# Two-layer vision tower on one core: the place of the square roots, the signed inverse and the selection in the first factorisation

## The reference, cut to what matters

```
p = unfold(x)                                  # 64 images, 51 patches of 64 x 25
h = gelu(p @ weight + bias)                    # C = 64 channels
n = layernorm(h)
q, k, v = split(n @ w_qkv.T + b_qkv)           # 8 heads of 8 channels
qgr, _ = qr(q);  kgr, _ = qr(k)                # per image and head: 51 x 8
grass = (qgr @ kgr.T) ** 2 * grassman_scale
dots  = q @ k.T
a = batchnorm(concat(dots * scale, dots ** 2 * riem_scale, grass))
a = softmax(conv_1x1(a))
h = h + (a @ v) @ w_proj.T + b_proj
h = h + mixture_of_experts(layernorm(h))       # 6 experts, the best 2
```

## Time and profile before

| | us |
|---|---|
| median of three runs (334.08 to 338.35) | 334.38 |
| the profiled execution, its own time | 336.93 |
| its span, from the first to the last instruction | 334.4 |
| TensorE matmul busy | 283.7 (85%) |
| VectorE busy | 201.1 (60%) |
| ScalarE busy | 172.0 (51%) |
| GpSimd busy | 70.5 (21%) |
| mean granted TensorE clock of the span | 0.911 |

### The profile page before, as it was taken

How to read it: one execution, slowest core, us unless ns; L and a number is a source line. 1 busy time by engine, 2 the same in 40 slices (tenths; PEclk the granted TensorE clock), 3 DMA queues, 4 the chain that set the end, 5 groups by cost and what they waited for, 6 DMA issues and landing times.

```text
span 334.4 us, 11326 instructions
## 1 busy us (share of the span) xinstructions
PE 283.7 (85%) x4854; PEld 199.1 (60%) x4854; DVE 201.1 (60%) x549; ACT 172.0 (51%) x310; POOL 70.5 (21%) x78
## 2 busy tenths in 40 slices
PE   4296999999788578595999999999876899998883
PEld 2176766877557467474788887886755453333331
DVE  1445087967477569788465466575587362465571
ACT  2445363342523156853566885666654565445731
POOL 8001114201103131132178322352200030000000
PEclk9787999999969879789599999999999899559999
DMA  8999960000000000000000000000000000010102
GB/s 226 284 297 269 251 159 2 5 3 4 0 2 2 5 2 2 2 2 2 4 3 4 4 4 2 2 6 2 4 2 0 2 1 2 1 25 2 25 0 50
DMA packets 16848, 13.88 MB, mean 42 GB/s; under 512 B 4128, under 2 KB 16416, under 8 KB 16800
## 3 DMA queue, kind: packets, MB, share of 16 engines
q1 hardware_dynamic: 16800, 13.18, 15.9%
HBM read 12.34 MB, written 0.84 MB: 39 GB/s over the span
## 4 chain that ended last, share of the span: by engine, by line
PE 63%; DVE 17%; ACT 8%; issue 7%; SPq 2%; DMA 2%; POOL 0%; ACTq 0%; DVEq 0%; POOLq 0%
PE banks L1149 10%; PE banks L1424 8%; PE banks L1408 6%; PE banks L1435 5%; PE banks L1449 4%; PE banks L1548 3%; PE banks L1583 3%; PE banks L1532 2%; PE banks L1569 2%; PE banks L1239 2%; DMA pixels<-in_x_dram 2%; PE banks L1155 2%; DVE pixels L918 2%; PE banks L1169 1%; PE banks L1209 1%
## 5 line engine op out<-in xcount | busy, mean ns | idle before, releaser
L1424 PE MATMUL banks<-pixels,convw 64*64 64x204 f32 x768 | 43.4, 358 | 9.9 <-DVE pixels L922 9.9
L309 POOL TENSOR_TENSOR qbd<-q,weights 128x448 f32<-128x448 f32 x32 | 31.4, 984 | 89.6 <-PE banks L1408 89.4
L1149 PE MATMUL banks<-pixels,taps 64*64 64x204 f32 x800 | 40.7, 355 | 9.2 <-DVE pixels L226 6.3
L1149 PEld LDWEIGHTS banks<-pixels,taps 64*64 64x64 f32 x800 | 32.3, 142 | 15.3 <-DVE pixels L226 7.0
L918 DVE TENSOR_REDUCE pixels<-banks 128x8 f32<-128x408 f32 x32 | 18.6, 583 | 35.9 <-PE banks L1424 33.8
L1424 PEld LDWEIGHTS banks<-pixels,convw 64*64 64x64 f32 x768 | 30.1, 143 | 14.5 <-issue 11.4
L1408 PE MATMUL banks<-kbd,qbd 64*64 64x102 f32 x1024 | 33.0, 270 | 2.9 <-issue 1.5
L1408 PEld LDWEIGHTS banks<-kbd,qbd 64*64 64x64 f32 x1024 | 26.3, 144 | 7.6 <-issue 4.3
L284 POOL TENSOR_TENSOR rstd<-var_eps,minus_half 102x8 f32<-102x8 f32 x8 | 13.1, 1639 | 77.2 <-DVE var_eps L710 77.1
L523 ACT ACTIVATE pixels<-banks 128x816 f32<-128x816 f32 x32 | 27.2, 851 | 0.0
L1449 PEld LDWEIGHTS banks<-vbd,pixels 115*51 115x51 f32 x512 | 15.7, 133 | 18.1 <-issue 13.5
(11 more groups left out here) (175 smaller groups left out, 505.0 us busy)
## 6 DMA issues: line engine op xcount, KB each, us to landing
pixels<-in_x_dram SPq DMA_DIRECT2D x16, 434.0 KB, 6.8
pixels<-in_x_dram SPq DMA_DIRECT2D x32, 108.5 KB, 6.9
out_dram<-pixels SPq DMA_DIRECT2D x8, 102.0 KB
weights<-in_w_dram SPq DMA_DIRECT2D x1, 652.0 KB, 8.8
weights<-in_w_dram SPq DMA_DIRECT2D x1, 564.0 KB, 7.8
taps<-in_w_dram SPq DMA_DIRECT2D x1, 416.0 KB, 3.5
```

Source lines behind the costliest of these rows:

```text
L309: pool.tensor_tensor(qbd[u][:, :].rearrange("p (c h i) -> p c h i", c=QB, h=H), qv.unsqueeze(2).to_broadcast([128, QB, H, NI]), w("headmas ...
L1149: last = nc.tensor.matmul(bank[r][64 * s:64 * s + 64, 0:2 * EN], tap(u, r), src, start=(u == 0), stop=(u == PW - 1))
L1424: last = nc.tensor.matmul(bank[2 + r][64 * to:64 * to + 64, 0:4 * N], convw[64 * r:64 * r + 64, k * HI:(k + 1) * HI], src[64 * r:64 * r + ...
```

## The change

Four edits, all around the first factorisation:

- ScalarE gets a new operation `load_roots()`: a square root of one constant column (`eps`) into a new tile `root` of 128 x 1, for which nothing waits. It stands behind `value_tokens(1)`.
- `pivot_roots(0)` moves from behind `center(2)` to ahead of `squares_ln(2)`, directly behind `load_roots()`.
- On VectorE `signed_inverse(0)` comes directly behind signs(7), ahead of `variance_eps(3)`. `variance_eps(3)` follows it, and `scale_ln(3)` moves behind `gram_blocks(8)` and `(9)`.
- On TensorE `select_q_and_k(0)` moves from behind gram(10) to ahead of `broadcast1(3)`.

```diff
+        root = sb("root", [128, 1])
...
+            def load_roots():
+
+                nc.scalar.activation(root[:, :], vec("eps"), ACT.Sqrt).then_inc(S["root_table"], 1)
+
             def pivot_roots(b):
...
             value_tokens(1)
+            load_roots()
+            pivot_roots(0)
             squares_ln(2)
             center(2)
-            pivot_roots(0)
             gelu(3)
...
                 elif j == 4:
                     scale_ln(2)
-                elif j == 6:
-                    variance_eps(3, 3)
-                elif j == 7:
-                    scale_ln(3)
             signed_inverse(0)
+            variance_eps(3, 3)
             gram_blocks(8)
             gram_blocks(9)
+            scale_ln(3)
             q_times_k(0)
...
             gram(9)
+            select_q_and_k(0)
             broadcast1(3)
             tokens(11)
             gram(10)
-            select_q_and_k(0)
             q_and_k(3)
```

More of the change, by code:

```diff
@@ L190, in vit_tower_kernel @@
             q_mm k_mm q_done k_done kbd_k tok_tr v_mm qk_tok_done v_tok_done
-            gram_mm gmask_done cgram_done atop_cp atop_mm g_mm aug_done elim pivots qr_pow lu linv_done sel_mm
+            gram_mm gmask_done cgram_done atop_cp atop_mm g_mm aug_done elim pivots root_table qr_pow lu linv_done sel_mm
             mstep z_mm ik_cp sel_cp z_cp bd_done kp_mm kp_done cvec_mm cvec
```

## The result

| | before | after |
|---|---|---|
| all runs beside each other | 22 runs, median 337.5 us (330.6 to 342.3) | 22 runs, median 331.52 us (326.9 to 336.48) |
| mean of all runs | 337.08 us | 331.41 us |
| the profiled execution | 336.93 us, span 334.4 | 329.21 us, span 326.6 |
| mean granted clock of that span | 0.911 | 0.909 |

The ratio is 0.9896, with a 95% interval of 0.985 to 0.9941: about 1% faster, and clear of no change. That ratio compares only the runs within 1.5% of each kernel's fastest (6 of 22 before, 12 of 22 after); the medians of all runs lie further apart, 331.52 / 337.5 = 0.982. Both are given, since part of the difference is time at the lower clock, and that is not the same in every run.

A forecast was written before the change was run, and what follows sets the result against it. VectorE's order in the first factorisation was taken as the bound; 1.6 (roots), about 3.1 (order) and 0.9 us (clock) made 5.6, discounted to 5.2: 329.2 us from a median of 334.38, range 325.5 to 332.9.

The forecast's parts named there:

- Roots 1.6: ScalarE's earlier pivot root starts VectorE 2.17 us earlier; 1.58 us remain at group 2's scaling, then held by its broadcast.
- The 3.1 of the order: Gain of about 3.1 us up to block_m(0) from reordering signed inverse, gram blocks and selection.
- the 0.9 of the clock: Gain of 0.9 us because TensorE's q and k of group 3 no longer last at half clock.
- The sum: block_m(0) 5.6 us earlier, 4.0 without the earlier half clock; at one in four, 5.2 us, giving 329.2 us.
- How the numbers follow: Range 325.5 to 332.9 us; chances 29% under 327.7, 68% within 2%, 3% above 341.1, only by a doubled E.
- E: Rival: the shift lowers the clock before the experts and keeps it down, up to 8.4 us lost, 337.6 us; 4%.
- Up to 73 us TensorE is simply full: Claim that before the first factorisation's stretch TensorE had no idle time, 41.30 busy of 41.30 us in a window.
- the shift reaches the end: Claim that the second factorisation, steps and experts wait for nothing absolute in time, so the 5.6 us carry through.
- rival C: Later half-clock stretches, from 112 us on, fall elsewhere: one fewer gives 325.9 us (20%), one more 332.5 us (8%).
- The constant's root: New ScalarE operation behind the early table load, priced at 0.20 us, able to gain nothing since nothing reads it.
- B: Rival: TensorE falls to half clock in the new place too; gain 3.6 us, 330.8 us; 12%.
- D: Rival: table switch costs 2.66 us instead of 1.28 (329.6 us), or the norms absorb the rest (332.8 us); 6% together.

The follow-up runs named there:

- e10: Kernel before with only ScalarE's new order (constant's and pivots' roots ahead of the third group's squares), run a second time; 332.15 us, a single execution.
- e5: Kernel before run once more, unchanged, for another trace; 338.72 us, a single execution; 24.94 us from the third group's variance to block_m(0).
- e7: Changed kernel without the constant's root and with the two waits of the Gelu operations swapped; 329.43 us median of 6, ratio 0.9763.
- e3: Changed kernel without load_roots(), the pivots' root still ahead of the squares; 332.03 us median of 4, ratio 0.9852.

## Why the prediction was right or wrong

- **The places of the events in the stretch: right.** Roots 2.17 earlier: 1.05 to -1.19 is 2.24. Scaling of group 2 moved by 1.58: 1.60, and held by the broadcast. Squares still in time for the variance: no idle time before it. Signed inverse within the idle time: 88.94 against 90.30. Selection ahead of the broadcast costs 0.25: 0.18. Product of q and k at 91.8 - 75.40 = 16.4 into the stretch: 16.18. `block_m(0)` at 20.47: 20.14. Gain against that trace 5.6: 5.92. One path was not as worked out: the columns' product, priced at 0.91 us from a row that was partly at half clock, took 0.74 and ended at 97.61, and `block_m(0)` waited for gram block 10 (97.31 and 0.63 us), which the prediction left out of that path. That the two end some 0.3 us apart, so that the number came out, is luck.
- **The shares in it.** Roots 1.6: 1.60, shown (e10 against before). The 3.1 of the order and the 0.9 of the clock can't be compared one by one, since the dip also lengthens the path in which the order's share was counted. Without any dip the forecast was 4.0 in all, so 2.4 for the order; e10 against the changed kernel gives 22.65 - 20.14 = 2.5, and the sum is 4.1. With the dip of the first trace the clock's whole share was 5.6 - 4.0 = 1.6; it was 1.8.
- **The step that failed is the discount in "The sum"**, which took the half clock of 94.4 to 101.0 to be missing in one execution of four and whole in the others, and so made 5.2 of 5.6 and 4.0. The clock's share in that forecast is 1.2 us. What the runs showed in its place: the dip was in all three traces of before, but of unequal length, and the gain in the stretch was 5.9, 4.8 (e5) and 5.9 us, while by the estimate of 24.25 us 4.1 are left without it. The ratio gives 1.04%, 3.5 us of 334.4 (0.6 to 1.5%, 2.0 to 5.0 us). The 4.1 us that don't rest on the clock lie inside, and at an equal clock whole executions also differ by 4.1; the forecast of 5.2 us, 1.6%, lies just above. The medians of all runs differ by 1.8%, 6.0 us; the 0.009 by which the mean clocks above differ would be 1.8 us of such a difference, an estimate, which leaves 4.2. That the single dip in the stretch is what moves the ratio wasn't shown, since only one execution of a kernel is traced at a time.
- **The base.** The 334.38 of three runs was low; 22 runs have a median of 337.5. So 331.52 us is 2.3 over the 329.2 forecast although the medians moved by 6.0 us and not by 5.2. That it lies in the range owes something to the range's width. In "How the numbers follow" the 3% above 341.1 have no row: E was priced at 337.6 and 4%.
- **"Up to 73 us TensorE is simply full": wrong.** It stood idle 2.62 us before the second embedding, behind the first Gelu's table load; e7 gets 1.34 of them back. From there (28.9) to 73 us it was busy 42.97 of 44.10 us.
- **That the shift reaches the end: right as far as can be seen.** From `block_m(0)` to the end of the span the kernel before took 232.9, 234.0 and 233.2 us, the changed one 228.7 and 232.7, and e3 and e7 in the same order 232.9 and 232.7. The 228.7 stands alone; it adds 4.2 us to the 7.8 by which the profiled pair differ in span, and the repeats don't give it to the change. It isn't rival C's "one fewer" dip: up to the last attention step's transposes the changed kernel took 154.52 us and that of before 157.93, both at a mean clock of 0.93, and behind them 74.21 and 74.97 at 0.85 and 0.86. So most of it is in the attention steps at the same amount of half clock, which lay earlier in them (up to 154.3 us instead of 165.9). Why that costs less wasn't followed further.
- **The constant's root: needless.** The prediction priced it at 0.20 and put the early table load ahead of it. It costs 0.11 (76.16 to 76.27), and the load starts just as early without it (e3): the move of `pivot_roots(0)` does all. The description of the kernel before says that a load stands behind its operation's wait; the traces show that only for the Gelu operations, which have two waits.
- **The rivals.** B didn't happen in five traces. D fell: the load again ended 0.01 us before the root (74.87 + 1.28 = 76.15, 76.16), without the drain that the Trainium skill ("ScalarE: Activation LUTs", "What ACT_TABLE_LOAD costs") adds to it. C stays open, as said above. E didn't happen: the clock was low from 253 to 263 us, where the changed kernel's experts begin (252.7), but came back, and at 265 to 285 it is full in both kernels.

## What to carry to other kernels

Where two in-order engines hand small work to each other, count each engine's idle time in one stretch and fill it with what is ready behind the waiting instruction: here two gram blocks and a signed inverse put into the wait for a norm, with the selection moved up for them, were worth more (2.5 us) than the earlier root (1.6 us). Before fetching a table by a dummy operation, look which wait the inserted load carries; with one wait the load already went ahead here, and with two the order of the waits decided. Where a run's time scatters by 1%, judge a change of that size by a stretch of the trace between two fixed events, in more than one execution, and keep apart what only the clock gave back.

## What the runs showed of the hardware

- A table load (1.28 us) isn't held by the wait that stays with the operation behind it: it started 0.27 us before the pivots were copied (e3), and 1.3 us before the embedding's end (e7). A second wait of that operation does hold it (82.42, behind the embedding's end).
- The same idle time of TensorE didn't always bring the lower clock, and not always for as long. Around the 1.15 us before gram(10) the dip of the kernel before lasted 6.8, 3.4 and 6.8 us; the 1.85 us before the third group's q and k brought none in these three traces, and the 1.84 and 1.85 us in the same place brought 3.4 us of it in each of the two traces of the order alone. Once at half clock, TensorE stayed there from 285.3 to 302.2 us although it was busy 16.82 of 16.90 us. What decides this was not found.
